# A two-layer hybrid network on one core: other stages for the expert layers' side work, one attention sum per block, reordered expert outputs

## The reference, cut to what matters

```python
x = x + lru(layernorm(x))                 # 1
x = x + ffn(layernorm(x))                 # 2
x = x + ssm(layernorm(x))                 # 3
x = x + ffn(layernorm(x))                 # 4
x = x + attention(layernorm(x))           # 5  16 heads of 32
x = x + moe(layernorm(x))                 # 6
x = x + linear_attention(layernorm(x))    # 7
x = x + moe(layernorm(x))                 # 8
```

```python
scores = einsum('bshd,bthd->bhst', q, k) * scale;  attn = softmax(scores)   # attention
out = einsum('bhst,bthd->bshd', attn, v) @ Wo.T + bo

probs = softmax(x @ router_weight.T)                                        # moe, 64 experts
topw, topi = top_k(probs, 8);  topw = topw / topw.sum(-1)
# every expert takes up to 256 of its tokens, in token order
g, u = split(xe @ gate_up_proj[e]);  ye = (silu(g) * u) @ down_proj[e]      # 512 -> 2*192 -> 512
y[token] = sum over its experts of topw * ye
```

## Time and profile before

| | us |
|---|---|
| median of 3 runs | 5405.37 (5400.83 to 5413.63) |
| the profiled execution | 5397.6 |
| its span | 5395.9 |
| PE busy in the span | 4767.6 |
| attention heads, about 1281 to 2287 | 1006 |
| atte, 2287 to 2347 | 60 |
| moe1: logits 2347 to 2417, routing to 2488, experts to about 3097 | 70, 71, 609 |
| moe2: logits 4611 to 4683, routing to 4752, experts to about 5360 | 72, 69, 608 |

### The profile page before, as it was taken

How to read it: one execution, slowest core, us unless ns; L and a number is a source line. 1 busy time by engine, 2 the same in 40 slices (tenths; PEclk the granted TensorE clock), 3 DMA queues, 4 the chain that set the end, 5 groups by cost and what they waited for, 6 DMA issues and landing times. The chain is left out here.

```text
span 5395.9 us, 66202 instructions
## 1 busy us (share of the span) xinstructions
PE 4767.6 (88%) x26222; PEld 2548.7 (47%) x26224; DVE 2412.7 (45%) x3331; ACT 1633.7 (30%) x2761; POOL 1532.6 (28%) x953
## 2 busy tenths in 40 slices
PE   7367997899999999967999869999999989589996
PEld 3133433333333333245666536666666654366663
DVE  7854778366666666634222223333333321332222
ACT  5414553212555546702111122222222210121110
POOL 1010000003777764012555401111111110045553
PEclk9688998999999999978999989999999999699998
DMA  2000000100000000044999720000000031459997
GB/s 70 0 2 19 6 0 2 33 0 1 1 1 1 1 1 1 3 165 115 246 253 254 170 76 25 29 30 30 30 22 30 24 105 62 169 163 253 245 254 201
DMA packets 237103, 417.66 MB, mean 77 GB/s; under 512 B 30992, under 2 KB 119056, under 8 KB 236816
## 3 DMA queue, kind: packets, MB, share of 16 engines
q1 hardware_dynamic: 179472, 270.89, 14.5%
q0 software_dynamic: 57344, 142.64, 12.2%
HBM read 297.53 MB, written 115.93 MB: 77 GB/s over the span
## 5 line engine op out<-in xcount | busy, mean ns | idle before, releaser
L2284 PE MATMUL linb_pr_ps<-lin_z,linb_wt 128*128 128x512 f32 x1536 | 679.3, 596 | 16.4 <-POOL linb_slope_own L2254 16.4
L1460 ACT ACTIVATE attc_prob<-attc_ps 128x512 f32<-128x512 f32 x1024 | 548.9, 597 | 438.2 <-PE attc_ps L1371 435.4
L1484 DVE TENSOR_REDUCE attc_peak<-attc_ps 128x2 f32<-128x1024 f32 x384 | 469.7, 1226 | 252.3 <-PE attc_ps L1379 252.3
L1334 POOL TENSOR_TENSOR attc_acc<-attc_acc,attc_prob 128x2048 f32<-128x2048 f32 x120 | 547.9, 4566 | 114.2 <-ACT attc_prob L1460 102.3
L1371 PE MATMUL attc_ps<-att_q,att_k 32*128 32x512 f32 x2048 | 529.2, 616 | 0.0
L2284 PEld LDWEIGHTS linb_pr_ps<-lin_z,linb_wt 128*128 128x128 f32 x1536 | 287.0, 192 | 342.8 <-issue 326.2
L1379 PE MATMUL attc_ps<-att_k,att_q 32*128 32x512 f32 x1536 | 447.1, 659 | 0.0
L2460 DVE SCALAR_TENSOR_TENSOR linb_gated<-linb_osb,linb_norm_w,linb_proj 128x512 f32<-128x512 f32 x64 | 94.4, 1474 | 668.0 <-ACT linb_osb L2387 668.0
L2261 POOL TENSOR_TENSOR linb_sq<-linb_osb 128x512 f32<-128x512 f32 x64 | 70.0, 1094 | 1041.4 <-ACT linb_osb L2387 1041.4
L1009 DVE TENSOR_TENSOR_SCAN ssmb_state<-ssmb_decay,ssmb_bu 128x2048 f32<-128x2048 f32 x64 | 279.8, 4410 | 78.8 <-ACT ssmb_decay L956 78.8
L1392 PE MATMUL attc_ps<-attc_prob,att_v 128*32 128x256 f32 (+1 forms) x3472 | 313.2, 433 | 0.3 <-ACT attc_prob L1460 0.3
(11 more groups left out here) (480 smaller groups left out, 7671.1 us busy)
## 6 DMA issues: line engine op xcount, KB each, us to landing
moe1w_wgu<-in_L_ffn_gate_up_proj SPq DMA_DIRECT2D x32, 1536.0 KB, 10.4
moe2w_wgu<-in_L_ffn_gate_up_proj SPq DMA_DIRECT2D x32, 1536.0 KB, 10.5
moe1w_wd<-in_L_ffn_down_proj SPq DMA_DIRECT2D x32, 512.0 KB, 13.7
gated_features<-linb_gated SPq DMA_DIRECT2D x64, 256.0 KB, 2.3
moe2w_wd<-in_L_ffn_down_proj SPq DMA_DIRECT2D x32, 512.0 KB, 13.6
linc_gt<-gated_features SPq DMA_DIRECT2D x7, 2048.0 KB, 8.2
linb_wt<-in_L_attn_b_qkv_w SPq DMA_DIRECT2D x16, 768.0 KB, 4.7
residual_rows<-residual SPq DMA_DIRECT2D x2, 4096.0 KB, 13.3
```

What stands on the lines that cost most here:

```text
L1334: pool.tensor_tensor(acc[:, n % 2, :, :], before, prob[:, U % NP, :, :], ALU.add).then_inc(pool_done, 2 if at == 1 else 1)
L1460: nc.scalar.activation(prob[:, U % NP, h, :], ps[:, n % 3 if at < 0 else at % 6, :], ACT.Exp).then_inc(exp_done, 1)
L1484: V.tensor_reduce(peak[:, w // TT % 2, i % QH, 2 * hp:2 * hp + 2, b], ps[:, bank:bank + 2, :], axis=AX.X, op=ALU.max).then_inc(mx_used, 1)
L2284: last = nc.tensor.matmul(pr_ps[:, use % 2, :], wt[:, b, kind, k, :], z[:, k, t * NB:(t + 1) * NB], start=(k == 0), stop=(k == DT - 1))
```

## The change

- Stage atte and stage linc save x to the first row buffer themselves, four tiles at a time as these are finished (SP waits for the last save before the stage ends). `moe_logits` no longer does.
- The zeros of the second row buffer are written in the second ffn stage for moe1 and at the start of `linear_heads` for moe2, as 16 DMAs of 256 KB from one tile that POOL clears.
- `moe_logits` finds each tile's top eight and replaces them right after the copy of its logits; the loads of the first weights are issued at the start of `moe_routing`.
- Attention: `SUMMED = (14, 15)`. There is one sum for each block, POOL or DVE adds 13 times for each block instead of 11, and DVE inverts straight from PSUM.
- Experts: one PSUM bank for the transposes, four for the outputs; `outer` does its four 128-row matmuls first and then its four tails.

```diff
@@ project_and_add (atte), and the same four saves in linear_outputs (linc)
             sp.wait_ge(loaded, 16)
+            for i in range(0, TT, 4):
+                sp.wait_ge(summed, i + 4)
+                sp.dma_start(g.y_dram[0][i * P:(i + 4) * P, :].rearrange("(i p) d -> p i d", p=P), g.X[:, i:i + 4, :]).then_inc(x_saved, 16)
+            sp.wait_ge(x_saved, 16 * (TT // 4))
@@ ffn(..., clear), and the same in linear_heads behind sp.wait_ge(consts, N_CONSTS)
+            if clear:
+                sp.wait_ge(blank, 1)
+                for i in range(TT):
+                    sp.dma_start(g.y_dram[1][i * P:(i + 1) * P, :], nothing[:, :]).then_inc(cleared, 16)
+                sp.wait_ge(cleared, 16 * TT)
@@ attention_heads
-        SUMMED = (7, 8, 14, 15)
+        SUMMED = (14, 15)
@@ sums (PE)
-                sources = [prob[:, (n - 1) % NP, :, :], prob[:, n % NP, :, :]]
-                if kind == "F":
-                    sem, count = summed_by(n - n % TT + POOLED[-1])
-                    pe.wait_ge(sem, count)
-                    sources.append(acc[:, n // TT % 2, :, :])
+                sem, count = summed_by(n - n % TT + POOLED[-1])
+                pe.wait_ge(sem, count)
+                sources = [prob[:, (n - 1) % NP, :, :], prob[:, n % NP, :, :], acc[:, n // TT % 2, :, :]]
@@ sums_out (DVE)
-                if kind == "Z":
-                    dve.wait_ge(z_done, 2 * n + 1)
-                    V.tensor_copy(zsum[:, :], ps[:, bank, :]).then_inc(mx_used, 1)
-                    return
-                dve.wait_ge(z_done, 2 * n + 2)
-                dve.wait_ge(mx_used, use_at[U, "F"])
-                V.tensor_tensor(tot[:, :], ps[:, bank, :], zsum[:, :], ALU.add).then_inc(mx_used, 1)
+                dve.wait_ge(z_done, n + 1)
+                V.reciprocal(tot[:, :], ps[:, bank, :]).then_inc(mx_used, 1)
                 dve.wait_ge(mx_used, use_at[U, "F"] + 1)
-                V.reciprocal(tot[:, :], tot[:, :]).then_inc(sum_step, 1)
-                dve.wait_ge(sum_step, n + 1)
@@ moe_logits (SP)
-            sp.dma_start(g.y_dram[0][0:T, :].rearrange("(i p) d -> p i d", p=P), g.X[:, :, :]).then_inc(x_saved, 16)
-            sp.wait_ge(blank, 1)
-            for i in range(0, TT, NB_ROWS):
-                sp.dma_start(g.y_dram[1][i * P:(i + NB_ROWS) * P, :].rearrange("(i p) d -> p i d", p=P), nothing[:, :, :]).then_inc(x_saved, 16)
...
-            for j in range(PW):
-                load_pair(sp, j)
@@ moe_logits (DVE)
-            for i in range(TT + NZ):
-                if i >= NZ:
+            for i in range(TT + NZ + 2):
+                if i >= NZ + 2:
+                    dve.wait_ge(top_done, i - NZ - 1)
+                    nc.vector.match_replace(others[:, i - NZ - 2, :], best[:, i - NZ - 2, :], logits[:, i - NZ - 2, :], -3.0e38).then_inc(others_done, 1)
+                if NZ + 1 <= i < TT + NZ + 1:
+                    dve.wait_ge(lg_used, i - NZ)
+                    nc.vector.max(best[:, i - NZ - 1, :], logits[:, i - NZ - 1, :]).then_inc(top_done, 1)
+                if NZ <= i < TT + NZ:
@@ moe_routing (SP), and its DVE loses the two loops of max and match_replace
+            for j in range(PW):
+                load_pair(sp, j)
             sp.wait_ge(share_ready, 1)
@@ moe_experts
-        xt_ps = L.ps("xt_ps", [P, 2, DT, P])
+        xt_ps = L.ps("xt_ps", [P, DT, P])
-        ye_ps = L.ps("ye_ps", [P, 3, D])
+        ye_ps = L.ps("ye_ps", [P, 4, D])
@@ transposes (PE)
-                if n >= 2:
-                    pe.wait_ge(xt_ready, n - 1)
+                if n >= 1:
+                    pe.wait_ge(xt_ready, n)
@@ outer (PE)
                     for x in range(2):
                         y = 4 * j + 2 * s + x
-                        if y >= 3:
-                            pe.wait_ge(ye_ready, y - 2)
-                        nc.tensor.matmul(ye_ps[:, y % 3, :], h[:, j % 2, x, cols], wd[:, j % PW, x, :], start=True, stop=False)
+                        if y >= 4:
+                            pe.wait_ge(ye_ready, y - 3)
+                        nc.tensor.matmul(ye_ps[:, y % 4, :], h[:, j % 2, x, cols], wd[:, j % PW, x, :], start=True, stop=False)
+                for s in range(2):
+                    cols = slice(s * P, (s + 1) * P)
                     for x in range(2):
```

More of the change, by code:

```diff
@@ L766, in _ @@
         def _(pool):
+            pool.memset(nothing[:, :], 0.0).then_inc(blank, 1)
             pool.wait_ge(loaded, 16)
@@ L1440, in _ @@
                 for kind in uses_of(U):
-                    if kind in "ZF":
+                    if kind == "F":
                         sums(U, kind)
@@ L1620, in _ @@
                     sp.dma_start(z_rows[:, r * NZ + b, :], z[:, b, :]).then_inc(z_saved[b], 16)
-            for j in range(PW):
-                load_pair(sp, j)
             for b in range(NZ):
                 sp.wait_ge(z_saved[b], 16 * (TT // NZ))
-            sp.wait_ge(x_saved, 16 * (1 + TT // NB_ROWS))
-        @block.gpsimd
-        def _(pool):
-            pool.memset(nothing[:, :, :], 0.0).then_inc(blank, 1)
         @block.vector
@@ L1763, in _ @@
             link = Chain(dve, chain)
-            for i in range(TT):
-                V.max(best[:, i, :], logits[:, i, :]).then_inc(chain, 1)
-            link.n = TT
-            for i in range(TT):
-                dve.wait_ge(chain, i + 1)
-                V.match_replace(others[:, i, :], best[:, i, :], logits[:, i, :], -3.0e38).then_inc(chain, 1)
-            link.n = 2 * TT
-            dve.wait_ge(chain, link.n)
             link(V.tensor_tensor(taken[:, :, :], others[:, :, :], logits[:, :, :], ALU.not_equal))
@@ L2171, in linear_heads @@
         sq = L.sb("sq", [P, NB])
+        nothing = L.sb("nothing", [P, D])
         gated = L.sb("gated", [P, 2, NB])
@@ L2224, in _ @@
                          allow_slow_non_contiguous=True).then_inc(norm_loaded, 16)
+            sp.wait_ge(consts, N_CONSTS)
+            for i in range(TT):
+                sp.dma_start(g.y_dram[1][i * P:(i + 1) * P, :], nothing[:, :]).then_inc(cleared, 16)
             with sp.Fori(0, PAIRS_L // 2 - 1) as r:
@@ L2250, in _ @@
             link(pool.memset(squares[:, :], 0.0))
+            link(pool.memset(nothing[:, :], 0.0))
             for h, s in enumerate(head_slopes()):
```

69 lines of the change are left out of this document (33 added, 36 removed).

## The result

| | before | changed |
|---|---|---|
| median of 4 runs each, us | 5409.15 (5400.83 to 5413.63) | 5315.06 (5309.18 to 5319.04) |
| span of the profiled execution | 5395.9 | 5312.3 |

The account below looks back on a forecast made before the run. PE bounds the experts; late z saves hold the logits stages, and ACT waits for PE in attention. -47 - 10.5 + 9 - 15 + 4.5 - 10 - 7 = -76 gave 5329 beside the median, taken as 5325; range 5290 to 5360.

Parts of the forecast that it names:

- Logits stages and the head of the routing stage: moe1 and moe2: z saves keep up, 44.0 us a stage, -47; maxima and replacements leave routing, -10.5.
- The saves of x: Ends of atte and linc: SP waits for the last 1 MB save, landing in 4.3 us; +4.6 each, +9.
- Weight loads in the routing stage: Routing: 9.4 MB of first weights take 29 us of about 66, share save still in time; 0 taken.
- `outer`: Experts: 5.89 us falls to 5.66, 0.23 saved in each of 63 to 64 outers; -15, ends 0 and -29.
- tails 2 x 1.06 = 2.12: Experts' `outer`: the second pair of tails cannot load weights under the first, so the pitch of 1.06 stays.
- the dense case: Experts' `outer`: four tails run dense, 4 x 0.431 = 1.72 and one change in place of 2.12; -29 end.
- The matmuls of `outer`: Experts: 8 x 0.431 + 0.09 = 3.54 us; a fourth bank removes the 0.15 us weight-load wait.
- rival B: Less comes: weight loads hold up the share save (+10), POOL's debt costs 3.2 us a block (+20); about 5350, chance 0.13.
- One bank for transposes, and the last outer: Experts: PE waits for ACT's copy at each stage's start, +1.5, and in the last outer, +0.7; +4.5 together.
- rival C: Slower: PE waits for ACT's copy in each of 256 transposes of both expert layers; about 5505, chance 0.05.
- Attention: Without Z, -1.7 and -0.5 a block, POOL's debt +1.4: -10 over 12 blocks; group 3, where DVE adds, -7.
- Rival A: More comes: tails run dense (-14), no POOL stall (-17), the clock gives a part; about 5292, chance 0.17.

Follow-up runs that it names:

- (a): Changed kernel with three repairs, this one saving the last 1 MB of x in the logits stage behind four z saves: 5299.46 us in one execution.
- (b): Same 5299.46 us execution; this repair to the changed kernel sends early expert transposes through empty output banks: 579.1 us to last output matmul, against 582.5 and 582.6.

## Why the prediction was right

The time (5315) lies 10 us under the forecast 5325; most mechanisms were those of the sum, one was wrong (how tails follow each other), and the clock had no term in attention. Against the medians the sum of -76 is 18 us short of the measured -94, against the profiled executions 7.6 short of -83.6.

- **Logits stages and the head of the routing stage** (-57.5 forecast, -63.7 measured): the pair pitch of 5.21 and 2.3 us for the end gave 44.0; moe2 took 43.7. The 6 us more are the clock's rise in moe1, which the forecast had as a bonus of 0 to 13 and put at 0, and named as a sign of being wrong. It could have been put at a few us: over ten executions it gave 0 to 14 in a stage.
- **The saves of x** (+9.2, measured +8.4): the interpolated landing of 4.3 us was measured as 4.3, and (a) took it back.
- **Weight loads in the routing stage** (0, measured -0.7): right, and the issuing time that they had cost in the logits stage is the 20.7 us seen with the loads back.
- **`outer`** (-15, measured -27.6): the step that failed is "tails 2 x 1.06 = 2.12". A pair's 1.06 holds 0.85 of work and 0.2 of change of kind, and four tails pay the 0.2 once: 1.92. I had the dense case as an end of the range and took the other because of the rule of the Trainium skill ("TensorE: Matmul & The Clock Gate", Part 3, The mechanism) that a weight load overlaps matmuls in flight only when its row group differs. The traces do not bear it out. In the run with the other order of tails, the loads for the third pair of passes start with the second pair (2754.53), whose passes fill both halves of the rows. The earlier trace rows had it before the result: loads over all 128 rows busy 9.55 of 10 us in which PE, with passes over all 128 rows, had no gap. The prediction's "the trace agrees so far as a pair goes" read two tails that start together as two in a row.
- **The matmuls of `outer`** (forecast 3.54, measured 3.53) came out with a wrong term: of the 0.15 that I gave to the bank, the bank gave 1.7 us a stage, 0.05 per pair, and the other 0.1 was change of kind, which the new order saves as well. That the sum held is luck.
- **The dense end of the range**, -29, does not follow from its own terms: 1.72 and a change of 0.09 in place of 2.12 are 0.31 for each of 63 to 64 outers, -20 beside the -15, and so -35. With the 0.2 that a change costs it is -28, about what was measured. In the same way rival B's extras of 10 and 20 us lead to 5355 and not to 5350. Neither changes the range.
- **One bank for transposes, and the last outer** (+4.5 together, measured +11.7): the starts were under-sized. The changed kernel has three waits of 0.77 at once and one more later in the first pair, 3.1 us, and (b) took back 3.4, not 1.5. In the steady order no wait appeared, so rival C fell; the ends' +3.3 and +1.6 varied between executions (+1.5 to +3.3, +1.6 to +2.1) and are not explained.
- **Attention** (-17, measured -12.2): the POOL debt was right in place and size (1.67 for 1.4), the block at full clock 0.75 shorter for 0.8. What the sum lacked is a term for the clock: the stretches at 0.95 to 0.98 in the windows of before were there to be read, and they moved with the edits of attention. The forecast of -0.8 a block was for full clock, and came out at 0.62 on average, 6.8 us over eleven blocks; what lies behind them gave 5.4, where -7 was forecast for group 3 alone.
- Rival A was half true (12.6 us more from `outer`, where it had 14, and some clock; POOL's stall came all the same). B's collision in the routing stage, C and D did not come.

The errors of `outer` (-12.6) and of the clock (-6) on one side, of the experts' starts and ends (+7) and attention (+5) on the other, cancel to about two thirds. The right total owes that much to luck.

## What to carry to other kernels

When an engine with a longer pitch than its producer loses its breathing space, compute when its last item is done against when the slot is wanted; one slot more in the ring was worth 28 to 32 us here, more than twice the change it belonged to. A stage that ends with a barrier pays for everything its DMA queue must still issue: put long issuing (20.7 us for 9.4 MB) where another engine's chain is longer. Matmuls of one height belong together; each change of kind cost about 0.2 us here. And before you say that two instructions do or do not run at once, look at their starts one by one: a merged line of the timeline hides them.

## What the runs showed of the hardware

- Two float32 passes over 64 rows, one in each half of the rows, start within 0.02 us of each other, and the next two 0.42 to 0.43 us later, the distance of passes over 128 rows. So such matmuls cost half (0.24 against 0.44 us a pass on average, the changes of kind included) because two run at once; one without a partner was not seen in these experts. PE found the partner behind another tail in its list, and reported the ends in the order of the list.
- Each change between passes over 128 and over 64 rows cost about 0.2 us, in either direction.
- Weight loads ran beside passes in the same rows (9.55 us of loads in 10 us of PE without a gap).
- A pause of PE at a block's start (2.24 us busy of 4) was followed by a granted clock of 0.50 for several us in one block and by none in the block before it. The same code's attention took 1004.6 and 1010.6 us, and with 0.7 us more of DVE work there it took 30 us more in one execution.
- PE can be busy without a gap in its record and yet stay at 0.50 for 40 us (moe2's logits stage, 43.6 to 43.8 in seven of ten executions); the same work in the other executions left it 7 to 28 us after the first transposes, and in moe1 13 to 33.
